# One core of a Mamba-2 and feed-forward kernel: y_diag of two tiles in a row, in every second step

## The reference

```python
xdt = xc * dtc[..., None]
scores = einsum('bclhn,bcshn->bchls', Cc, Bc) * Lmat       # Lmat: exp of differences of cs, lower triangle
Ydiag = einsum('bchls,bcshp->bclhp', scores, xdt)
states = einsum('bclhn,bchl,bclhp->bchpn', Bc, decay_states, xdt)
# prev: the states carried from chunk to chunk
Yoff = einsum('bclhn,bchpn,bchl->bclhp', Cc, prev, exp(cs))
Y = Ydiag + Yoff + x * D
yg = Y * silu(gate); out = yg * rsqrt(mean(yg**2 over the group)) * norm_w;  s = out @ out_proj_w.T
```

## Time and profile before

| what | value |
|---|---|
| median of 3 runs | 1774.01 us (1773.98 to 1774.44) |
| the profiled execution | 1773.51 us, its span 1771.7 us |
| granted clock, mean | 0.999 |
| TensorE busy | 1757.7 us, 99% |
| VectorE / GpSimd / ScalarE busy | 1436.6 (81%) / 1262.6 (71%) / 1227.7 (69%) |

### The profile page before, as it was taken

How to read it: one execution, slowest core, us unless ns; L and a number is a source line. 1 busy time by engine, 2 the same in 40 slices (tenths; PEclk the granted TensorE clock), 3 DMA queues, 4 the chain that set the end, 5 groups by cost and what they waited for, 6 DMA issues and landing times.

```text
span 1771.7 us, 30224 instructions
## 1 busy us (share of the span) xinstructions
PE 1757.7 (99%) x10297; PEld 1455.5 (82%) x10297; DVE 1436.6 (81%) x2211; ACT 1227.7 (69%) x2456; POOL 1262.6 (71%) x877
## 2 busy tenths in 40 slices
PE   8999999999999999999999999999999999999999
PEld 7788888888888888888888888888888888888877
DVE  7978888888889788888788888888887888868941
ACT  6986777777776777777867787677777787643320
POOL 5677787777777787777777787778776877676630
PEclk9999999999999999999999999999999999999999
DMA  6433333243333343333333342333333343235522
GB/s 203 161 125 102 100 132 106 96 122 107 118 108 111 97 137 97 99 113 123 113 107 102 112 130 90 117 102 119 118 101 101 115 125 94 78 109 167 151 77 95
DMA packets 122595, 202.83 MB, mean 114 GB/s; under 512 B 23057, under 2 KB 60561, under 8 KB 122193
## 3 DMA queue, kind: packets, MB, share of 16 engines
q1 hardware_dynamic: 120720, 197.32, 35.5%
q10 hardware_dynamic: 1728, 3.65, 0.5%
HBM read 193.57 MB, written 7.34 MB: 113 GB/s over the span
## 4 chain that ended last, share of the span: by engine, by line
PE 96%; DVE 2%; POOL 1%; issue 1%; DMA 0%; SPq 0%; ACT 0%; POOLq 0%; DVEq 0%
PE bank L135 17%; PE bank L137 17%; PE bank L136 17%; PE bank L546 11%; PE bank L588 7%; PE bank L634 6%; PE bank L636 6%; PE bank L635 6%; PE bank L833 3%; PE bank L695 3%; DVE z L1191 0%; PE bank L677 0%; PE bank L657 0%; DVE x_in L1348 0%; POOL yt L1529 0%
## 5 line engine op out<-in xcount | busy, mean ns | idle before, releaser
L1525 POOL TENSOR_TENSOR yt<-yt,ec 128x384 f32<-128x384 f32 x128 | 174.7, 1365 | 307.2 <-DVE ec L1260 307.2
L1191 DVE SCALAR_TENSOR_TENSOR z<-bank,cw_all,z 128x511 f32<-128x511 f32 (+2 forms) x477 | 356.1, 747 | 11.6 <-ACT z L946 0.4
L907 ACT ACTIVATE lm<-lm,hp 128x128 f32<-128x128 f32 x1024 | 313.2, 390 | 0.8
L135 PE MATMUL bank<-xn_hi,conv_hi 128*128 128x512 f32 x640 | 261.0, 408 | 3.6 <-DVE z L1191 3.5
L1225 DVE SCALAR_TENSOR_TENSOR lm<-lm,gm 128x1024 f32<-128x1024 f32 x128 | 260.9, 2038 | 3.5 <-ACT lm L907 3.5
L1251 DVE TENSOR_TENSOR xdt<-bank,hp 128x512 f32<-128x512 f32 x128 | 88.3, 690 | 201.1 <-PE bank L695 201.0
L137 PE MATMUL bank<-xn_hi,conv_lo 128*128 128x512 f32 x640 | 250.9, 392 | 0.0
L136 PE MATMUL bank<-xn_lo,conv_hi 128*128 128x512 f32 x640 | 250.6, 391 | 0.0
L1529 POOL TENSOR_TENSOR yt<-yt,gate 128x512 f32<-128x512 f32 x128 | 227.1, 1774 | 19.0 <-POOL yt L1525 0.9
L1534 POOL TENSOR_TENSOR conv_lo<-raw_x,conv_hi 128x512 fp32r<-128x512 f32 x124 | 219.0, 1766 | 9.7 <-ACT conv_hi L846 9.6
L135 PE MATMUL bank<-xn_hi,gate_hi 128*128 128x512 f32 x512 | 212.4, 415 | 0.0
(11 more groups left out here) (147 smaller groups left out, 3945.4 us busy)
## 6 DMA issues: line engine op xcount, KB each, us to landing
lm<-cs_d SPq DMA_DIRECT2D x128, 512.0 KB, 4.0
raw_x<-w_conv_dram SPq DMA_DIRECT2D x128, 256.0 KB, 3.0
ec<-e_d SPq DMA_DIRECT2D x256, 96.0 KB, 3.7
raw_o<-w_out_dram SPq DMA_DIRECT2D x64, 256.0 KB, 2.7
raw_g<-w_gate_dram SPq DMA_DIRECT2D x61, 256.0 KB, 2.7
raw_b<-w_conv_dram SPq DMA_DIRECT2D x32, 256.0 KB, 3.4
q_raw<-w1q_dram SPq DMA_DIRECT2D x10, 256.0 KB, 3.8
q_s<-w1s_dram SPq DMA_DIRECT2D x10, 256.0 KB, 4.0
```

Of the source, the lines that this page charges most:

```text
L135: pe.matmul(dst, a_hi, b_hi, start=(i == 0), stop=False)
L907: e = act.activation(lm[m % 3][:, u, :], lm[m % 3][:, u, :], ACT.Exp, bias=hp[bd.seq][:, Q_CS, k1, u:u + 1])
L1191: dve.scalar_tensor_tensor(dst[:, d:SEQ], src[:, 0:SEQ - d], cw_all[:, bd.group, pos, 3 - d:4 - d], dst[:, d:SEQ], ALU.mult, ALU.add).then ...
```

## The change

In the steps of tiles 4 to 119 (`paired(n)`), an even step issues no y_diag. The odd step issues both: tile n-1 into ps_y, then tile n into ps_x, the bank from which xdt and xw of tile n have been read. The gate product follows, and then the state product, once VectorE has read y_diag of tile n out of ps_x. VectorE does both y1 in the odd step, and the x taps before the state there. GpSimd, in odd steps, does the add and gate product of tile n-1 after its weight parts, and y_lo ahead of the sum of squares; ScalarE copies the gate ahead of y_hi and square there. xdt has two tiles, lm four. To make room, z has two tiles instead of three (B and C are convolved in place in b_t and c_t), sq is gone (squares are written into the used gate tile), and raw_b is gone: B/C weights land in raw_g or raw_o, and SyncE issues that load last in its step, with waits for those tiles.

```diff
+LM_BUFS = 4
+def paired(n):
+    return TILES // 2 <= n < TILES * (BODIES - 1)
...
-        raw_b = alloc(main, "raw_b", [DIM])
-        z = alloc(main, "z", [3, SEQ])
+        z = alloc(main, "z", [2, SEQ])
-        sq = alloc(main, "sq", [SEQ])
+        xdt1 = alloc(main, "xdt1", [NC * P])
...
+        def bc_tile(body, i):
+            return b_t[:, :] if i == 0 else c_t[:, body.seq, :]
+        def bc_raw(body):
+            if body.n == 0:
+                return lm[3][:, 0:NC, :].rearrange("p c l -> p (c l)")
+            return raw_g[:, :] if body.seq else raw_o[:, :]
+        def sq_tile(kp):
+            return sq_sum[:, :] if kp == 0 else gate[:, kp % 4, :]
...
 # SyncE
-                    wait(sp, yd_done, m - 2)
+                    wait(sp, yd_done, m - LM_BUFS + 1)
...
+                for nb, i in bc_piece(body, k + 1):
+                    wait(sp, wlo_b, 2 * nb.n + i)
+                    if nb.seq:
+                        sp.wait_ge(wlo_g, 8 * body.group + 8)
+                    else:
+                        sp.wait_ge(wlo_o, TILES * body.group + TILES)
+                    sp.dma_start(bc_raw(nb), w_conv[nb.group, BC_POS[i]]).then_inc(rawb_in, 16)
...
 # TensorE
-                    pe.wait_ge(y1_done, n)
+                    pe.wait_ge(y1_done, n - 1 if paired(n) and k % 2 else n)
...
+            def diag(n, dst):
+                pe.wait_ge(xdt_done, n + 1)
+                pe.wait_ge(sc_done, n + 1)
+                for c in range(NC):
+                    for j in range(2):
+                        mm = pe.matmul(dst[HD * j:HD * j + HD, c * P:(c + 1) * P],
+                                       xdt[n % 2][:, c * P + HD * j:c * P + HD * j + HD],
+                                       lm[n % LM_BUFS][:, NC * j + c, :], start=True, stop=True)
+                mm.then_inc(yd_done, 1)
+            def two_diags(body, k):
+                n = TILES * body.n + k
+                pe.wait_ge(t0_done, n)
+                diag(n - 1, ps_y)
+                pe.wait_ge(xw_done, n + 1)
+                diag(n, ps_x)
...
+            def state_mm(body, k):
...
                     pe.wait_ge(xw_done, n + 1)
+                    if paired(n) and k % 2:
+                        pe.wait_ge(y1_done, n + 1)
...
+                if paired(TILES * body.n + k) and k % 2 == 0:
+                    state_mm(body, k)
+                    gate_mm(body, k)
+                    out_mm(body, k)
+                elif paired(TILES * body.n + k):
+                    two_diags(body, k)
+                    gate_mm(body, k)
+                    state_mm(body, k)
+                    out_mm(body, k)
...
 # ScalarE
+                    if (m - 4) % TILES:
+                        wait(act, sqa_done, (TILES - 1) * ((m - 4) // TILES) + (m - 4) % TILES)
                     act.activation(gate[:, kg % 4, :], gate_bank(body, k)[:, :], ACT.Copy).then_inc(gev_done, 1)
...
+                gate_first = paired(n) and k % 2
+                if gate_first:
+                    gate_raw(body, k)
...
+                if not gate_first:
+                    gate_raw(body, k)
...
 # VectorE
-                    wait(dve, yd_done, n)
-                    dve.tensor_tensor(by_head(xdt[:, :]), by_head(ps_x[:, :]),
+                    wait(dve, yd_done, n - 1)
+                    dve.tensor_tensor(by_head(xdt[n % 2][:, :]), by_head(ps_x[:, :]),
...
+                if body.exists() and not paired(n):
+                    inner(k, ps_y)
+                elif paired(n) and k % 2:
+                    inner(k - 1, ps_y)
+                    inner(k, ps_x)
+                    taps_x_conv()
...
 # GpSimd
+                chain_late = paired(n) and k % 2
...
+                if pv.exists() and not chain_late:
+                    gated()
...
+                if paired(n) and k == 0:
+                    sum_sq()
...
+                if chain_late:
+                    gated()
-                low_first = (body.is_number(BODIES - 1) and k >= 5) or body.is_number(BODIES)
+                low_first = (body.is_number(BODIES - 1) and k >= 5) or body.is_number(BODIES) or chain_late
```

More of the change, by code:

```diff
@@ L200, in build @@
         gate = alloc(main, "gate", [4, SEQ])
-        lm = [alloc(main, f"lm{i}", [2 * NC, CHUNK]) for i in range(3)]
+        lm = [alloc(main, f"lm{i}", [2 * NC, CHUNK]) for i in range(LM_BUFS)]
         hp = [alloc(main, f"hp{h}", [NQ, TILES, 2 * NC]) for h in range(2)]
@@ L292, in build @@
         hp_in = [sem(f"hp_in{i}") for i in range(2)]
-        row_in = [sem(f"row_in{i}") for i in range(3)]
+        row_in = [sem(f"row_in{i}") for i in range(LM_BUFS)]
         ec_in = [sem(f"ec_in{i}") for i in range(2)]
@@ L442, in step @@
                     wait(sp, wlo_o, TILES * group + pos)
+                    if group > 0 and pos == 0:
+                        sp.wait_ge(wlo_b, 2 * bd.n + 2)
                     if group == 0 and pos == 0:
@@ L583, in y_diag @@
                     wait(pe, t0_done, n)
[L584 to L591, removed]
+                    diag(n, ps_y)
+                    state_mm(body, k)
+            def state_mm(body, k):
+                n = TILES * body.n + k
+                if body.exists():
                     pe.wait_ge(xw_done, n + 1)
+                    if paired(n) and k % 2:
+                        pe.wait_ge(y1_done, n + 1)
                     if k == 0:
@@ L684, in sum_squares @@
                             pe.matmul(ss[:, c:c + 1], sq_sum[:, o], one[:, :], start=True, stop=False)
-                            mm = pe.matmul(ss[:, c:c + 1], sq[:, o], one[:, :], start=False, stop=True)
+                            mm = pe.matmul(ss[:, c:c + 1], sq_tile(TILES - 1)[:, o], one[:, :], start=False, stop=True)
                     mm.then_inc(ss_mm, 1)
@@ L853, in raw_bc @@
                     act.wait_ge(bp_done, 2 * nx.n + i + 1)
-                    if not nx.is_number(0):
-                        wait(act, bs_done, 2 * nx.n + i)
+                    if i == 0:
+                        wait(act, bt_mm, nx.n)
+                    else:
+                        wait(act, yo_done, TILES * (nx.n - 1))
                     pos = BC_POS[i]
-                    act.activation(z_bc(nx, i), ps_g[:, :], ACT.Identity, scale=cw_all[:, nx.group, pos, 3:4],
+                    act.activation(bc_tile(nx, i), ps_g[:, :], ACT.Identity, scale=cw_all[:, nx.group, pos, 3:4],
                                    bias=cw_all[:, nx.group, pos, 4:5]).then_inc(tap0_b, 1)
@@ L931, in silu_bc @@
                 act.wait_ge(taps_b, 3 * (2 * nx.n + i) + 3)
[L932 to L937, removed]
+                act.activation(bc_tile(nx, i), bc_tile(nx, i), ACT.Silu).then_inc(bs_done, 1)
             def raw_x_conv(body, k):
@@ L1271, in step @@
                 if k in (4, 5) and nx.exists():
-                    taps(nx, BC_POS[k - 4], z_bc(nx, k - 4), ps_g, tap0_b, taps_b, 2 * nx.n + k - 4)
+                    taps(nx, BC_POS[k - 4], bc_tile(nx, k - 4), ps_g, tap0_b, taps_b, 2 * nx.n + k - 4)
                 if k == 2 and before.exists():
@@ L1321, in step @@
                     ins.then_inc(st_done, 1)
-                bd, kx = at(body, k, 3)
-                if bd.exists():
-                    taps(bd, X_POS[kx], z[:, kx % 2, :], ps_a, tap0_x, taps_x, TILES * bd.n + kx)
+                if not (paired(n) and k % 2):
+                    taps_x_conv()
                 if n == 1:
```

77 lines of the change are left out of this document (40 added, 37 removed).

## The result

The changed kernel takes 1761.88 us (median of 6 runs, 1760.22 to 1765.26) against 1773.99 us before (6 runs, 1773.67 to 1774.44): a ratio of 0.9936, 95% interval 0.9925 to 0.9946. It is 12.1 us faster; 18.5 were forecast. Its runs spread over 5 us, those of before over 0.8. The execution that was profiled is a long one, 1765.14 us with a span of 1763.3, so its waits are more than those of the median run.

A forecast was written before the change was run, and what follows sets the result against it. TensorE's own order was taken to bound the kernel. 58 pairs saving 0.43 us each give 24.9, less 6.4 of added waits: 18.5 off 1774.0 makes 1755.5 us, range 1747 to 1769.

The forecast's parts named there:

- second group 0.87: On TensorE in odd steps, a second y_diag group directly behind the first costs 0.87 us, not 1.02.
- State product 0.67 behind a split matmul: On TensorE, the state product no longer follows a 64-column group and costs 0.67 us instead of 0.86.
- rival 2: The extra 0.19 us belongs to the state product itself and goes along with it: 1771.7 us; chance 0.06.
- D = 0.10: Surcharge on the gate product behind the 64-column group in odd steps: 0.10 us, bounded by 0 and 0.19.
- a sum of 19.7 to 24.9: Saving in us of TensorE's order over 58 pairs, with the gate product's surcharge at 0.19 to 0.10, never 0.
- Waits, 6.4: All waits the change adds on TensorE, in steps 3 and 4: 6.4 us together.
- Step 4: The gate product waits for VectorE's taps of B: 0.15 us, 15 times, 2.2 us.
- Step 3: y_diag waits for t0, 0.1 us 14 times; in first sequences the state product waits for y1, 0.4 in 7 bodies.
- DMA at nothing: On SyncE's queue, ec and weight loads behind the add go 3 to 5 us later in odd steps; costed at nothing.
- the signs that it named: Right: TensorE's chain over 95%, small VectorE waits at steps 3 and 4. Wrong: gate copy or DMA releasing TensorE.
- Rival 1: The ring through VectorE, GpSimd, ScalarE and TensorE sets the pair, making the state product wait: 1791 us; chance 0.11.
- Rival 3: Gate product's surcharge is 0.19, and ring or ScalarE takes another 0.1 to 0.15 a pair: 1764 to 1769; chance 0.07.

The follow-up runs named there:

- the last kernel: Changed kernel with ec's load last, t0 ahead of xw in step 3, taps first and GpSimd's chain last in step 4, gate's weights earlier: 1758.22 us, ratio 0.9909.
- the opposite arrangement: The kernel before, without pairs, with the state product behind the gate product and VectorE's x taps ahead of the state: 1784.76 us, ratio 1.0062.
- three edits more: Changed kernel with ec's load last, t0 ahead of xw in step 3, taps of B ahead of t0 and GpSimd's chain last in step 4: 1758.54 us, ratio 0.9918.

## Why the prediction was right, and where its terms were off

The direction, the mechanism and the range (1747 to 1769) held. The time was 6.4 us above the forecast, and that by the order on TensorE (7.0 too much), less 0.6 by the waits. By its steps:

- **y_diag, second group 0.87.** Right: 1.90 for both.
- **State product 0.67 behind a split matmul.** Right in both steps; rival 2 is refuted. An even step was to be 1.21 shorter and is 1.16 to 1.22 in the last kernel.
- **D = 0.10.** The term that was mis-sized. It is 0.20, shown in the changed kernel and, in the opposite arrangement, in the kernel before. The argument for 0.10 was that a split matmul is long enough to hide the second half of the surcharge. It hides nothing of it: half is a gap ahead of the first instruction, half is on the second, just as on the short float32 instructions. Of the two bounds at hand, the higher was the only one measured behind the group, and was the one to take. 0.10 x 58 = 5.8 us.
- **A return that was not counted.** The odd step goes back from a float32 product to split matmuls three times instead of twice. Behind the group that costs 0.02 us beside D: 1.2 us in 58 pairs. With D and this the pair should save 0.53 - 0.20 - 0.02 = 0.31, as steps 2 and 3 of the last kernel show. The order gives 17.9 us and not 24.9.
- The Trainium skill ("TensorEngine Tiling (Array Packing)", Key Properties) says that changing the tiling mode drains the engine. The prediction took from it a sum of 19.7 to 24.9. The 0.20 agrees with the rule, and lies 0.01 above the bound that gave 19.7; that and the return take the order below the sum.
- **Waits, 6.4.** In the median run they are 17.9 - 12.1 = 5.8, so the sum was near. Its parts were not all right, and that the sum came out near is in part luck. The profiled run, 3.3 us above the median, has 7.3 us in tiles 4 to 119 (and 1.65 ahead of the first body's projection of B): 2.4 in steps 4 and 5, 4.2 in step 3, and 0.7 in hundredths in steps 6 and 7. Step 4 was forecast at 0.15 x 15 = 2.2: there the wait was 0.17 in all 15 bodies, which cost the pair of steps 4 and 5 0.16. Step 3 was forecast at 4.2 in 21 small waits; it lost 4.2 in four bodies. y_diag waiting for t0 was to be 0.1 in 14 bodies and came at 0.4 in two, where the scores ran beside GpSimd's sum of squares. The state product in step 3 of first sequences was to be 0.4 in 7 bodies and came at 1.3 and 1.4 in two. It isn't the silus and the table load that are late there by themselves, but a weight load in front of them.
- **DMA at nothing.** Wrong: one load landed 2.4 us too late for ScalarE in two bodies of the profiled run, a late landing being what the forecast itself named as the condition to watch. Of the signs that it named, the chain has 88% TensorE and not over 95%, with a DMA in it (2%), and the gate copy releases TensorE once, in the first body (1.5 us). With ec's load last the load goes out 2.4 us earlier and these waits are gone. That this queue also makes the spread of 5 us is not shown: the spread was 1.5 with ec's load last, but 3.3 with that and three edits more.
- **Rival 1**, the ring through four engines, set none of the 58 pairs; its links show in single bodies, where a load was late or the scores ran long. **Rival 3** had D right and put another 0.1 to 0.15 a pair on top of the 6.4 us of waits; no such wait came. With D = 0.19 and 6.4 of waits its own sum would have been 1760.7.

## What to carry to other kernels

Where a surcharge has one measured row and one argument for less, the row is the forecast. Count the switches of instruction kind on the bounding engine before and after, all of them, not only those that the edit is about. Ahead of moving an instruction up or down on one engine, follow what it releases on the next queue, and see what stands behind that there: one reversed pair on VectorE cost 23 us until GpSimd's order was changed with it, and then gave 0.12 us a step. And where two engines slow each other, a cover of a few tenths can hold in one body and fail in the next by which of them starts first.

## What the runs showed of the hardware that was not expected

- Leaving the 64-column weights costs 0.19 to 0.20 us whoever comes next, a float32 product of 128 columns or a split matmul twice as long.
- After a float32 product of 128 columns, nine of the next eleven split matmuls come some 4 ns further apart than the 227 ns of the rest, 0.04 us in all; after the 64-column group 0.02.
- VectorE's two 128x1024 passes over a decay tile took 1.19 to 1.23 us when no GpSimd instruction was in flight at their start, and 1.2 to 2.3 when one was (on average 1.9 before, 1.8 in the changed kernel). Before, 203 of the 256 passes started beside one, in the changed kernel 166. GpSimd's add of 128x384 took 1.02 us beside VectorE's taps, which read a bank, and 1.5 to 1.6 on average, up to 2.0, beside the first of those passes. With fewer such meetings the busy sums of the two engines fell by 33.5 and 29 us. The account of the time above does without that; but single meetings did cost TensorE time, in bodies 10 and 12.
